# Latent attention with its softmax sums taken by a wider V on TensorE, and normalizations turned by row tiles

## The reference, cut to what matters

```
q = x @ q_w + q_b                                   # 16 heads of 32
k, v = split(concat(ctx, x) @ kv_w + kv_b)          # 1024 + 512 = 1536 keys
w = softmax(q @ k.T / 32, masked)                   # [512 rows, 1536 keys] for each head
acc = x + (w @ v) @ out_w + out_b
y = acc * rsqrt(mean(acc^2) + eps) * postnorm_w     # then the MLP
# elsewhere: y = (x - mean) * rsqrt(var + eps) * scale + offset
```

## Time and profile before

| what | value |
|---|---|
| median of 3 runs | 4511.32 us (4495.92 to 4513.83) |
| the profiled execution's own time | 4514.29 us |
| its span, first to last instruction | 4512.5 us |
| mean granted TensorE clock | 0.935 of 2.4 GHz |
| PE busy | 3995.1 us (89%) |
| DVE busy | 2751.4 us (61%) |
| ACT busy | 1878.4 us (42%) |
| POOL busy | 1509.8 us (33%) |

### The profile page before, as it was taken

The page is one execution under the profiler, slowest core; times in us unless marked ns, Lnnn a source line. Parts: engine busy times, 40 slices in busy tenths (PEclk is TensorE's granted clock), DMA queues, the critical chain, the costliest instruction groups (busy, mean ns, idle before and its releaser), DMA issues.

```text
span 4512.5 us, 55800 instructions
## 1 busy us (share of the span) xinstructions
PE 3995.1 (89%) x21018; PEld 2988.1 (66%) x21018; DVE 2751.4 (61%) x4218; ACT 1878.4 (42%) x3302; POOL 1509.8 (33%) x1514
## 2 busy tenths in 40 slices
PE   6899699997999989877878996999979999898878
PEld 5655488886888867443665554888868888674436
DVE  2588556556565564776525885565565655647765
ACT  2487344333443331444124883344333443224431
POOL 1543213223132223555216422133131331326552
PEclk9999799998999999887888997999989999998879
DMA  1211101011010122111223101011010110221202
GB/s 66 61 36 20 45 29 43 22 38 42 26 43 24 35 61 80 45 42 22 77 75 70 30 18 47 26 43 34 26 43 26 43 35 25 66 75 45 48 16 87
DMA packets 167577, 195.65 MB, mean 43 GB/s; under 512 B 18627, under 2 KB 123272, under 8 KB 167310
## 3 DMA queue, kind: packets, MB, share of 16 engines
q1 hardware_dynamic: 142734, 151.15, 10.9%
q0 software_dynamic: 24576, 40.94, 4.7%
HBM read 149.02 MB, written 2.10 MB: 33 GB/s over the span
## 4 chain that ended last, share of the span: by engine, by line
PE 68%; DVE 16%; ACT 5%; issue 5%; POOL 2%; DVEq 1%; DMA 1%; POOLq 1%; SPq 0%; ACTq 0%
PE ps L146 17%; PE ps L148 16%; PE ps L147 16%; PE ps L1167 4%; PE ps L781 3%; DVE w_pt_lo L1299 3%; DVE w_mx L1282 3%; PE ps L1672 2%; PE ps L793 2%; DVE h_pt L1796 2%; PE ps L1682 1%; PE ps L1654 1%; DVE h_mxs L1778 1%; PE ps L769 1%; POOL g_qs L651 1%
## 5 line engine op out<-in xcount | busy, mean ns | idle before, releaser
L1088 POOL CAST w_wo_hi<-w_raw 128x1024 fp32r<-128x1024 f32 x32 | 35.1, 1096 | 1322.7 <-PE ps L148 1322.7
L1299 DVE TENSOR_TENSOR w_pt_lo<-ps,w_pt_hi 128x512 fp32r<-128x512 f32 x512 | 334.9, 686 | 157.5 <-ACT w_pt_hi L1233 157.5
L1730 ACT ACTIVATE h_pt<-ps,zero_col 128x512 f32<-128x512 f32 x384 | 256.6, 687 | 296.5 <-PE ps L1682 289.7
L1233 ACT ACTIVATE w_pt_hi<-ps 128x512 fp32r<-128x512 f32 x512 | 281.5, 596 | 200.8 <-PE ps L1167 200.8
L906 DVE CUSTOM_DVE_ANT_0 g_units<-ps,g_mask 128x1024 f32<-128x1024 f32 x256 | 311.3, 1218 | 81.3 <-PE ps L769 81.3
L1282 DVE TENSOR_REDUCE w_mx<-ps 128x1 f32<-128x1024 f32 x256 | 312.0, 1219 | 31.4 <-PE ps L148 30.6
L1167 PE MATMUL ps<-ident,w_p 128*128 128x128 f32 x2048 | 279.0, 275 | 39.7 <-DVE w_pt_lo L1299 39.7
L781 PE MATMUL ps<-ident,g_units 128*128 128x128 f32 x2048 | 293.1, 285 | 20.0 <-ACT g_turned L860 17.9
L1778 DVE TENSOR_REDUCE h_mxs<-ps 128x1 f32<-128x512 f32 x384 | 241.2, 681 | 100.7 <-PE ps L1672 100.4
L852 ACT ACTIVATE g_units<-g_units,g_nmx 128x1024 f32<-128x1024 f32 x256 | 294.5, 1150 | 17.7 <-DVE g_nmx L906 15.0
L1167 PEld LDWEIGHTS ps<-ident,w_p 128*128 128x128 f32 x2048 | 235.3, 140 | 96.6 <-DVE w_pt_lo L1299 67.3
(11 more groups left out here) (358 smaller groups left out, 10757.0 us busy)
## 6 DMA issues: line engine op xcount, KB each, us to landing
w_raw<-in_L_xattn_wk SPq DMA_DIRECT2D x32, 512.0 KB, 3.4
w_raw<-in_L_xattn_wq SPq DMA_DIRECT2D x32, 512.0 KB, 3.5
w_raw<-in_L_xattn_wv SPq DMA_DIRECT2D x32, 512.0 KB, 3.6
w_raw<-in_L_xattn_wo SPq DMA_DIRECT2D x32, 512.0 KB, 3.6
mlp_raw<-in_L_xattn_w_fc SPq DMA_DIRECT2D x64, 256.0 KB, 3.1
mlp_raw<-in_L_xattn_mlp_w SPq DMA_DIRECT2D x64, 256.0 KB, 3.2
h_ks<-h_k_hi POOLq DMA_DIRECT2D x64, 192.0 KB, 3.0
g_qs<-g_q_hi POOLq DMA_DIRECT2D x256, 32.0 KB, 1.9
```

The costliest lines, as they stand in the source:

```text
L1233: act.activation(pt.h[:, x[2] % 4, :], ps[:, T_BANK + tn % 2, :], ACT.Copy).then_inc(t_hi, 1)
L1299: dve.tensor_tensor(pt.l[:, x[2] % 4, :], ps[:, T_BANK + tn % 2, :], as_f32(pt.h[:, x[2] % 4, :]), ALU.subtract).then_inc(t_free, 1)
```

## The change

Four parts:
- **V with a column of ones.** `vd` holds for every key tile and head 32 columns of V and one column of ones. `v_and_one` hands PE 64 columns from there (V, the ones, and 31 columns of the next head that nobody reads). A burst is now two pairs of matmuls: two tiles go to partitions 0 to 63 and 64 to 127. The sums over keys land beside the product. `dve_z`, `pool_z` and `zs` are gone. `zq` and `fold` both multiply `parts` by a block of `folds`, and `zq` starts at j = 4 in place of 5.
- **Norms turned by row tiles.** Each of the four row tiles is turned as soon as it is normalized, into four banks. Two of the four banks go through DVE (scale and shift, L1902 of the new kernel) and then ACT, two through ACT twice. In the first norm, scale and shift are folded into the two passes that normalize.
- **`Turn` has four banks** in place of two.
- **Semaphores are merged** in `wide` (one `split` for four, two `loaded` for four) and `mlp` (one `own_d`); the order of the instructions stays.

```diff
-            vd = sb(own, tag + "_vd", [P, KT, D])
+            vd = sb(own, tag + "_vd", [P, KT * HEADS * VW + DH])
...
-            S_IN, PV_AT, TAIL = (2, 1, 2, 2, 2, 1, 2), {5: 0, 9: 1}, 2
+            S_IN, PV_AT, TAIL = (2, 1, 2, 2, 2, 1, 2), {5: (0, 1), 9: (2, 3)}, 2
+            PAIRS, PV_LATE = KT // 2, (4, 5)
...
+            def v_and_one(st, hd):
+                return vd[:, (st * HEADS + hd) * VW:(st * HEADS + hd) * VW + 2 * DH]
...
-                for j in range(4):
-                    st = 4 * i_ + j
-                    i = pe.matmul(ps[32 * j:32 * j + 32, O_BANK, :], vd[:, st, hd * DH:(hd + 1) * DH],
-                                  pt[:, tile_at(st), :], start=i_ == 0, stop=i_ == 2, skip_group_check=True)
+                for j in range(2):
+                    i = pe.matmul(ps[64 * j:64 * j + 64, O_BANK, :], v_and_one(2 * pair + j, hd),
+                                  pt[:, 2 * pair + j, :], start=pair == 0, stop=pair == PAIRS - 1, skip_group_check=True)
...
-                                act.wait_ge(pv_done, (m - 1) * 3 + j // 4 + 1)
-                                if j < HALF:
-                                    act.wait_ge(z_dve, m * 3 - (2 if j < 3 else 0))
-                                else:
-                                    act.wait_ge(z_pool, (m - 1) * 6 + max(j - HALF, 1))
+                                act.wait_ge(pv_done, (m - 1) * PAIRS + j // 2 + 1)
...
-                        if j == 9 and 0 <= n < HEADS:
-                            dve_z(dve, b, n)
...
+                pool.memset(vd[:, 0:KT * HEADS * VW].rearrange("p (h n) -> p h n", n=VW)[:, :, DH:VW], 1.0)
```

More of the change, by code:

```diff
@@ L1100, in pool_ @@
                             pool.tensor_tensor(row[:, :], row[:, :], raw_of(i, name)[:, h, :], ALU.add)
-                        pool.drain().then_inc(split[name], 1)
+                        pool.drain().then_inc(split, 1)
                 pool.tensor_copy(row_p.h[:, :], row[:, :])
@@ L1361, in latent @@
             first.close()
[L1362 removed]
+            pt = sb(own, tag + "_pt", [P, KT, NQ])
             first = ExitStack()
@@ L1848, in norm @@
             gb = sb(own, tag + "_gb", [P, 2, D]) if first else None
-            turn_n = Turn(xn, XT, scale=c_scale, shift=c_shift, tmp=tmp)
             rows_ld = sem(tag + "_rows_loaded") if first else None
             var_done, sqrt_done, xn_done = (sem(n) for n in ("var_done", "sqrt_done", "xn_done"))
+            turned, by_act, by_dve = (sem("norm_" + x) for x in ("turned", "by_act", "by_dve"))
             rounds = 2 if first else 1
@@ L1856, in norm, with run, affine @@
             done = new_barrier(3)
+            BY_ACT = 2
+            def run(b):
+                return b * norms[0] + nth
+            def affine(c):
+                return (cols[:, c_scale + c:c_scale + c + 1],
+                        zero_col[:, :] if c_shift is None else cols[:, c_shift + c:c_shift + c + 1])
             def sp_(sp, b):
@@ new lines, in act_ @@
+                for c in range(KC):
+                    sc, sh = affine(c)
+                    if c >= BY_ACT:
+                        act.wait_ge(by_dve, run(b) * (KC - BY_ACT) + c - BY_ACT + 1)
+                        act.activation(XT.h[:, c, :], tmp[:, c, :], ACT.Copy).then_inc(by_act, 1)
+                    else:
+                        act.wait_ge(turned, run(b) * KC + c + 1)
+                        act.activation(XT.h[:, c, :], ps[:, T_BANK + c, :], ACT.Identity, bias=sh,
+                                       scale=sc).then_inc(by_act, 1)
+                        act.activation(tmp[:, c, :], ps[:, T_BANK + c, :], ACT.Identity, bias=sh,
+                                       scale=sc).then_inc(by_act, 1)
@@ new lines, in act_, with moments @@
+                barrier(act, done, b)
+            def moments(dve, b, r, e):
+                if rms:
+                    for lt in range(LT):
+                        dve.tensor_tensor_reduce(xn[:, lt, :], src[:, lt, :], src[:, lt, :], 1.0, 0.0, ALU.mult,
+                                                 ALU.add, ve[:, lt:lt + 1])
+                    dve.drain()
+                    dve.tensor_scalar(ve[:, :], ve[:, :], 1.0 / D, float(e), ALU.mult, ALU.add).then_inc(var_done, 1)
+                else:
+                    for lt in range(LT):
+                        dve.bn_stats(stats[:, lt, :], src[:, lt, :])
```

233 lines of the change are left out of this document (97 added, 136 removed).

## The result

The changed kernel takes 4394.12 us (median of 4 runs, 4391.32 to 4401.39), the kernel before 4511.15 us (4 runs) on the same chip: a ratio of 0.9752, 95% interval 0.9737 to 0.9768. Forecast were 4365 us, with a range from 4322 to 4445. So the direction and the range hold, and 29 us of the forecast gain of 146 are missing. The profiled execution has a span of 4389.5 us against 4512.5, 123.0 us less.

A forecast was written before the change was run, and what follows sets the result against it. DVE's softmax sums were taken to stop PE in `latent` and lower its clock. Per batch 51.6 + 6 + 14.4 + 1.5 - 0.5 = 73 us, 146 in all, gave 4365 us, range 4322 to 4445.

The forecast's parts named there:

- What bounds the kernel: Head loop of `latent`: DVE's softmax sums delay the maxima; PE stops some 3 us a step, then runs at 1.2 GHz.
- (1): Head loop: `dve_z` and `pool_z` go, leaving DVE 8.2 us of maxima a step; DVE and ACT stay well under PE.
- (2): Head loop: a pair of 64-wide matmuls takes 0.99 us (bounds 0.50 and 1.98), adding 3.0 us of PE per head.
- rival D: Head loop: two 64-wide matmuls do not run beside each other, 1.98 us a pair; kernel 4555 us; chance 5%.
- (3): Head loop: step 0 as model, 9.8 us base plus pairs and projections: 254.6 us, 51.6 less a batch.
- (4): End of `latent`: step 15 takes 5 us less, PE's wait ahead of `zq` 1.8 less; together 6 us, rounded down.
- (5): Norms: turns by row tile and folded passes save 8.4 us in three norms, 6 in the first; 14.4 a batch.
- (6) to (8): `Turn` banks: 1.5 us less a batch; POOL's fills: at most 0.5 more; merged semaphores: nothing; `spread` wait could double.
- A: Head loop: PE sets it, at high clock nearly throughout; kernel 4365 us, own range 4335 to 4400; chance 60%.
- B: Head loop: PE's short stops keep the clock at 0.86; kernel 4468 us, half of it 4415; chance 17%.
- C: Head loop: added pairs cover waits for maxima and cost less than 0.99 us; kernel 4320 us; chance 13%.
- E: Head loop: `spread` DMAs or the reciprocal ahead of `fold` hold it near its old pace; 4440 to 4510 us; chance 5%.

The follow-up runs named there:

- narrow kernel: The changed kernel with three bursts of four 32-wide key tiles per head again, without the column of ones or any softmax sums: 4353.49 us, ratio 0.9658.
- half maxima: The changed kernel with each of DVE's maxima in the head loop taken over 256 of its 512 columns: 4369.43 us, ratio 0.9690.

## Why the prediction was right, and where it was wrong

**What bounds the kernel, and (1): right.** The sums held the loop. Without them PE's stops ahead of S go from 36.5 to 3.5 us and the clock from 0.86 to 1.00. DVE's and POOL's were taken out together, so the share of each stays open. Another place in the queue gave back a fifth of what they cost, 12 of 55 to 65 us a batch.

**(2), the pair: right in price, wrong in its share of the path.** A pair takes 0.94 us in a burst and 1.01 alone, 0.99 forecast; rival D is excluded, and the price is the one argued from the stream of 512 columns. The Trainium skill ("TensorEngine Tiling (Array Packing)", Theoretical Speedup) has up to 4x for a dimension of at most 32, up to 2x for one of at most 64. The trace agrees as far as the ratio of the two goes: four narrow matmuls in 1.00 us, two wide in 0.94. The "192 added bursts" at 190 us are a slip: three bursts become six a head, so 96 are added in both batches, 95 us, which is what the sum in (3) has. But 0.94 us of PE are not 0.94 us of the step: of the 44.6 us a batch, some 27 showed at the full clock (an estimate from the narrow kernel's full-clock steps), 24.2 in the second batch and 14.4 in the first, where the narrow kernel lost some of its clock.

**(3), the loop: the step that failed.** "Its projections take 12 x 0.233 = 2.8 us, so a step without any and with 2 bursts is 9.8 us." That subtracts PE's work from a step that PE did not set. The narrow kernel shows 12.6 us for such a step. At the full clock the base was too low by some 29 us over a loop, the price of the pairs too high by some 18. Much of the two cancels, and what is left is the miss of 10.6 us: that 254.6 came near 265.2 is in part luck. The bound below it in the forecast went the wrong way as well: it took the records' busy share of step 0 as PE's own work. What sets the steps with few projections is not one engine. S 3 to 12 goes partly at DVE's pace of 0.606 us (half maxima: 9 to 10 us a loop). In steps 6 and 10 PE stands 1.5 us each for `acc`, which is 3 of the 10.6 us missing if it shows in full. ST goes at ACT's pace behind a double burst. That this last part counts was read from the timeline, not shown; splitting the bursts did not bring what it promised, and five orders of the same work moved the loop by no more than -4.6 to +4.6 us.

**(4), the end of `latent`: right in sum, by other parts.** 5.8 and 6.6 us less, 6 forecast. But step 15 did not get shorter by 5 us: from the last row copy to the last burst's end it is 2056.14 to 2073.00, 16.9 us against 15.9 + 1.9 = 17.9 before, one of its double bursts at the low clock. So it gave 1.0 us. PE's wait ahead of `zq` gave 3.1 us, 0.79 in place of 3.90. The forecast's 5.83 us run from the start of the last burst and hold its 1.93 us; by that count it is 3.06 now. Some 1.7 us came behind that, where the clock is higher: `zq` takes 1.06 us in place of 1.94. These are the rows:

```profile
2062.68 3.31 PE L1627 MATMUL ps<-h_pt,h_vd 128*64 128x512 f32 x8
...
2070.73 2.27 PE L1627 MATMUL ps<-h_pt,h_vd 128*64 128x512 f32 x8
...
2073.79 1.06 PE L1601 MATMUL ps<-h_parts,h_folds 128*32 128x512 f32 x8 [0.79 <-ACT h_parts L1708]
```

**(5), the norms: mis-sized.** 17.4 us in place of 28.8. In the fourth it is 7.0 us from the last normalized tile (2097.89) to the last subtraction's end (2104.88), where 5.4 were forecast. The forecast costed one subtraction of 0.69 behind ACT; there are four in a row, 3.41 us, since two passes by DVE stand ahead of them in its queue. In the second all of it went to POOL: "in a norm nothing but POOL's splitting runs beside it, and it is done by then" is false there. POOL was beside them before too: the four subtractions stood between waits for ACT, and took 2.66 and 2.95 us by twos. Now they follow each other at 1.78 us, and the stage ends no earlier. PSUM took them out of it. In the first norm the second folded pass cost 8.21 us, as forecast (8.3), but the first now waits 1.22 us for the rows of scale and shift, and the normalizing pass behind both takes 7.04 us in place of 5.03, with POOL at work beside nearly all of it.

**(6) to (8).** The turn's banks gave some 3 us a batch in load. The turn ahead of `latent` is 0.9 us shorter (3.8 us in place of 4.7, 0.75 forecast), but with POOL's fills its first split comes 0.4 us later (6.93 us after the turn's start, 6.53 before), and turn and prologue together take 63.4 us against 63.7: next to nothing was won there. The DMAs of `spread` stop S for 1.8 us in place of 6.0. The merged semaphores were not tried apart.

**The rivals.** A came true with a smaller gain, inside its own range by 6 us. B's mechanism did not occur in the changed kernel's loop (every step reads 1.00), but does in the narrow one and in the two with pairs in the next head. C's mechanism did occur: the added pairs cover stops (some 27 us shown for 44.6 of work), and a pair costs 0.94; its 4320 us did not come, since the other steps' base was too low. D did not occur; of E the small waits are there, and the two for `acc`.

## What to carry to other kernels

Work taken out of a step shows what it cost there, and its product of count and length does not: before a step's time is split into an engine's parts, show that this engine sets it, by a run in which the part is gone. An engine in the trace that is busy for all of a stretch may still wait a little at each instruction; compare the distance from start to start with the shortest one seen. And when an instruction takes longer beside another engine's work, as DVE's subtractions did here, moving one operand to another memory can be worth more than moving the instruction.
